# The vision-tower kernel: the row scatters wait for the values matmuls of their step

## The reference, cut to what matters

```python
h = einsum('bnd,ed->bne', patches, W) + b
a = layernorm(h)
q, k, v = split(a @ W_attn + b_attn)            # q and k get rotary factors
att = softmax(where(causal, q k^T * D**-0.5, -inf))
h = h + (att @ v) @ W_proj + b_proj
x = layernorm(h); t = rmsnorm(x) * norm_scale
top_vals, top_idx = top_k(t @ gate_w.T + gate_b, 4)
w = softmax(top_vals)
y_e = swiglu(t @ mlp1_w[e].T + mlp1_b[e]) @ mlp2_w[e].T + mlp2_b[e]
h = h + x + sum over the four experts e of w_e * y_e
```

## Time and profile before

| | |
|---|---|
| median of 3 runs | 541.59 us (537.69 to 542.88) |
| the profiled execution, its own time | 542.0 us |
| its span in the profile | 540.2 us |
| mean granted TensorE clock | 0.903 |
| busy: PE / DVE / ACT / POOL | 440.9 / 298.8 / 310.8 / 256.9 us |

### The profile page before, as it was taken

One profiled execution on the slowest core, in us unless ns is written; L12 is line 12 of the kernel. 1 busy time (PEld: TensorE's weight loads), 2 busy tenths in 40 slices (PEclk: granted clock), 3 DMA queues, 4 the chain that ended last, 5 costly groups with the idle time before them and its releaser, 6 DMA issues.

```text
span 540.2 us, 14340 instructions
## 1 busy us (share of the span) xinstructions
PE 440.9 (82%) x3865; PEld 390.1 (72%) x3866; DVE 298.8 (55%) x964; ACT 310.8 (58%) x832; POOL 256.9 (48%) x303
## 2 busy tenths in 40 slices
PE   2888977878787767119999999999999999999910
PEld 2676756556665545108999999999999999999910
DVE  0467968878778665403555555555555555555510
ACT  1247656666556642016777777777777777777600
POOL 1114576667677556700346444444444444444332
PEclk9789999999997755558999999999999999999965
DMA  8965454565541111333234444444344444432211
GB/s 222 257 158 166 138 152 147 172 172 153 153 134 51 41 41 56 128 114 101 52 55 78 61 63 61 63 61 61 53 69 61 61 61 62 63 40 30 24 22 22
DMA packets 41914, 49.72 MB, mean 92 GB/s; under 512 B 6387, under 2 KB 33251, under 8 KB 41860
## 3 DMA queue, kind: packets, MB, share of 16 engines
q1 hardware_dynamic: 26452, 33.48, 23.1%
q0 software_dynamic: 14544, 14.94, 17.9%
q10 hardware_dynamic: 864, 0.65, 0.4%
HBM read 30.82 MB, written 18.23 MB: 91 GB/s over the span
## 4 chain that ended last, share of the span: by engine, by line
PE 57%; issue 9%; DVE 9%; ACT 6%; another core or an unknown queue 5%; DMA 4%; SPq 4%; POOL 4%; POOLq 1%; DVEq 0%; ACTq 0%
PE bank L594 21%; PE bank L616 14%; PE bank L602 11%; PE bank L574 3%; PE bank L422 2%; ACT k_spread L657 2%; ACT p_spread L639 2%; POOL routed_rows L1140 2%; DMA out_rows<-x_sb 1%; SPq L322 1%; DMA x_sb<-patches 1%; SPq L321 1%; DVE t_row L902 1%; POOL rstd L1131 1%
## 5 line engine op out<-in xcount | busy, mean ns | idle before, releaser
L594 PE MATMUL bank<-rT,w_now 128*128 128x128 f32 x948 | 124.0, 281 | 0.3 <-ACT rT L639 0.3
L594 PEld LDWEIGHTS bank<-rT,w_now 128*128 128x128 f32 x948 | 115.1, 193 | 5.2 <-ACT rT L639 0.5
L730 ACT ACTIVATE k_spread<-bank,w_now 128x128 f32<-128x128 f32 x237 | 69.9, 372 | 58.1 <-PE bank L602 58.1
L1077 DVE TENSOR_TENSOR v_sb<-bank,w_now 128x384 f32<-128x384 f32 x79 | 44.1, 558 | 101.4 <-PE bank L602 80.4
L639 ACT ACTIVATE w_now<-w_sb 128x1158 f32 x79 | 92.5, 1171 | 13.4 <-issue 7.9
L616 PE MATMUL bank<-w_sb,p_spread 128*128 x474 | 83.9, 327 | 0.1
L1196 POOL DMA_INDIRECT out_rows<-x_sb,wtok_sb x25 | 40.1, 1605 | 79.9 <-issue 33.0
L616 PEld LDWEIGHTS bank<-w_sb,p_spread 128*128 128x128 f32 x474 | 76.1, 190 | 0.5 <-issue 0.4
L1140 POOL DMA_INDIRECT routed_rows<-packet,row_i x64 | 63.5, 992 | 24.2 <-issue 22.5
L602 PE MATMUL bank<-rT,w_now 64*128 64x128 f32 x948 | 64.2, 282 | 0.0
L1090 DVE SCALAR_TENSOR_TENSOR p_spread<-k_spread,v_sb 128x384 f32<-128x384 f32 x79 | 44.2, 560 | 35.7 <-ACT k_spread L730 31.4
(11 more groups left out here) (174 smaller groups left out, 688.6 us busy)
## 6 DMA issues: line engine op xcount, KB each, us to landing
x_sb<-patches SPq DMA_DIRECT2D x16, 384.0 KB, 3.4
w_sb<-w SPq DMA_DIRECT2D x32, 192.0 KB
w_sb<-w SPq DMA_DIRECT2D x16, 288.0 KB
w_sb<-w SPq DMA_DIRECT2D x64, 48.0 KB
wtok_sb<-routed_rows SPq DMA_DIRECT2D x25, 106.0 KB, 2.0
out_rows<-h SPq DMA_DIRECT2D x16, 96.0 KB
wproj_sb<-routed_rows SPq DMA_DIRECT2D x10, 106.0 KB
x_sb<-routed_rows SPq DMA_DIRECT2D x10, 106.0 KB
```

The source lines that it names most:

```text
L594: last = mm(dst[:, c * P:(c + 1) * P], w[:, a:a + P], t[:, part, :], start=(start and c == 0), stop=(not start and c == ICH - 1))
L730: last = nc.scalar.activation(gate_act[b][:, a:a + P], ps_glu[b][:, a:a + P], ACT.Silu, bias=w1_now[b][:, GLU_B + c:GLU_B + c + 1], scale= ...
L1077: V.tensor_tensor(lin[b].rearrange("p (c t) -> p c t", c=ICH), ps_lin[b][:, 0:INNER].rearrange("p (c t) -> p c t", c=ICH), w1_now[b][:, LI ...
```

## The change

POOL's instructions stay the same and in the same order. In the steps in which stages 6, 3 and 2 all hold a tile (n = 6 to 17, 12 of the 16 tiles' scatters), POOL waits, ahead of the first of the four scatters, for `pv_done` of the tile at stage 3: the values matmuls that PE runs in the same step.

```diff
                 if tile(6) is not None and tile(2) is not None:
+                    if tile(3) is not None:
+                        pool.wait_ge(s["pv_done"], tile(3) + 1)
                     scatter(tile(6), (n - 6) % 2)
                 if tile(4) is not None:
                     inverse_root(tile(4), ssq[:], 1.0 / DIM, "ssq_ready", msq, "msq_ready", rms, "t_row_ready",
                                  "rms_ready")
                     residual(tile(4))
```

## The result

The changed kernel takes 565.22 us (median of 4 runs, 563.68 to 566.96) against 541.57 us for the kernel before in the same session: +23.7 us, ratio 1.045, 95% interval 1.0388 to 1.0512. Slower, as forecast, and by more than the 14 us of the forecast, inside its range of 546 to 567. The profiled execution's span is 565.3 us, 25.1 more than before. In the table of runs further down a median is of all runs, while a ratio leaves out the slow ones, over 1.5% above the fastest of the same kernel: two of four in split_scatters and in changed_again (whose profile is of a slow one), one of four in split_again.

The account below looks back on a forecast made before the run. The step time was taken as bound by a loop of POOL's scatters, rms, DVE's t_row, inverse roots and row_i. First scatter at 65.61, eleven 12.71 us periods, +1.2 clock, -1.5 at the end: +14.2, 556 us, range 546 to 567.

Parts of the forecast that it names:

- Scatters, rms, t_row, pT, p_spread, values, scatters: Loop through POOL, DVE and PE that the new wait closes: 12.71 us a period, against 11.55 before.
- 4.86 + 0.92 + 0.1: Terms on POOL and DVE: four scatters 4.86 us, scatter end to rms end 0.92, rms end to t_row 0.1.
- the 5.09 from `t_row` to values: Terms t_row start to pT end 2.52 us, to first p_spread copy 0.32, four copies 2.10, then 0.15 to values.
- 0.92 + 0.82 = 1.74: Terms from PE to POOL: values to their signal 0.92 us, signal to first scatter 0.82.
- the clock term: Last changed steps at the lower clock: values to yT 1.56 us instead of 0.92, 1.2 us for two steps.
- the clock falls early: Rival: PE idles more and gets 1.2 GHz sooner, up to 1.2 us a step, 567 us in all; chance 0.10.
- A clock of 0.50 long before 165 us: Sign that the prediction is wrong: PE's clock at 0.50 well ahead of 165 us, from where it averaged 0.67.
- The loop's own bounds: Period of the token steps that the wait governs: 12.0 to 13.3 us, with 12.7 taken; chance 0.75.
- The lateness: Claim that scatters make PE's values signal late: 2.8 to 5.1 us to yT beside them, 0.92 without scatters.
- the 4.6 us of `p_pair`'s waits: POOL's p_pair waits 4.6 us in five steps for DVE's rinv_own; the change was to remove this.
- The shift of 1.7 us in step n = 6: First changed step: first scatter moves from 63.89 to 65.61 us, after values and their signal.
- The last step's gain of 1.5 us: Behind the last changed step, p_pair no longer waits 1.41 us for rinv_own; about 1.5 us given back.

Follow-up runs that it names:

- split_scatters: Kernel before, no wait, with two of the four scatters ahead of msq, rms and residual and two behind them in steps 6 to 17: 534.93 us, ratio 0.9852.
- changed_again: The changed kernel run once more, unaltered, for a second profile: 557.49 us, ratio 1.0522 to the kernel before.
- split_again: Repeat, on another chip, of the kernel before with two scatters ahead of rms and two behind residual, no wait: 534.33 us, ratio 0.9879.
- filled_pe: Changed kernel plus 8 extra unused PE matmuls ahead of the t_row transposes in steps 6 to 17: 554.57 us, ratio 1.0205 to the kernel before.
- scores_wait: Changed kernel with its wait on the earlier scores_done of stage 2 in place of pv_done: 546.12 us, ratio 1.0055 to the kernel before.
- split_filled: Kernel before with two scatters ahead of rms, two behind residual, no wait, plus 4 extra PE matmuls ahead of t_row's transposes: 520.82 us, ratio 0.9935.
- before_filled: Kernel before, no wait, with 8 extra PE matmuls ahead of the t_row transposes in steps 6 to 17: 552.15 us, ratio 1.0188.

## Why the prediction was right, and what it mis-sized

- **The direction and the loop: right.** "Scatters, rms, t_row, pT, p_spread, values, scatters", summed to 12.71 us. Shown: 12.4 us where the clock stays up (filled_pe), 12.8 in the changed kernel's faster steps. The terms 4.86 + 0.92 + 0.1 measure 5.81, the 5.09 from `t_row` to values 4.89, and 0.92 + 0.82 = 1.74 measures 1.71. Each was within 0.2 us.
- **What failed is the size of the clock term.** I gave 1.2 us for two steps at the end in the forecast itself, and 0.10 to the rival "the clock falls early", with up to 1.2 us a step. The clock fell in about every second step from n = 7 on, at 1.6 us a step where whole, 10.2 us in all by the comparison with filled_pe. A clock of 0.50 long before 165 us was one of the signs of being wrong, and it came. That rival's price (567) was nearer than the forecast (556). I had taken PE's mean busy share (0.83 to 0.73) and not where its idle time would stand: in one piece of 2.6 us ahead of the `t_row` transposes.
- **How much of the hit is luck.** The loop's own bounds, 12.0 to 13.3 us a period, end at about 563 us; the measured mean is 13.36 and the time 565.2. It lies in the range only because the upper end took in part of the clock rival. Term by term, the forecast's 14.2 us become the profile's 25.1 by 3.8 for the late start, 0.2 in step n = 6, -3.1 for the loop (12.4 for 12.7, eleven times), 9.0 for the clock (10.2 for 1.2) and 1.0 behind the last changed step: the loop's error hid part of the clock's.
- **The lateness: shown only in part.** With the scatters behind the values, `yT` comes 0.92 us after them (up to 1.57 where the clock is lower) in all 12 steps. In scores_wait the signal is 3.2 to 3.9 us behind the values in the 8 steps whose scatters start 0.3 to 0.5 us behind them, and 1.3 to 1.6 us in the 3 whose scatters start 1.0 us or more behind. So without scatters beside the values the signals are on time. But split_filled has the scatters beside the values and the signal on time, so the scatters alone do not make it late. What else it takes is open.
- **What the lateness costs the kernel before: misread.** The prediction says that the loop does not pass through the late signals in most steps, and prices them at the 4.6 us of `p_pair`'s waits. But DVE, which has `t_row`, works in order, and its base add waits for a late signal too. In the step after n = 7 of the kernel before:

```profile
80.00 0.57 POOL L1131 TENSOR_TENSOR rms<-msq,power 128x1 f32<-128x1 f32 x1
80.48 0.35 DVE L986 TENSOR_TENSOR h<-h,bank 128x192 f32<-128x192 f32 x1 [2.93 <-remote]
...
81.82 0.18 DVE L864 TENSOR_TENSOR rinv_own<-rinv,cst 128x24 f32<-128x24 f32 x1
...
82.06 0.75 DVE L902 SCALAR_TENSOR_TENSOR t_row<-x,rms,nscale_bc 128x192 f32<-128x192 f32 x1
```

  `t_row` starts 1.49 us behind the end of `rms`. It is 0.57 to 1.95 us late in 8 of the 12 steps and 0.1 or less in four (not three, as the prediction has it), 10.6 us in all; in the changed kernel it is 0.04 or less in every step. The periods of the kernel before are 10.8 to 11.2 us where `t_row` is on time, and 11.2 to 12.7 where it is not. An estimate: 127.0 us less eleven periods of 10.8 is 8 us that signals on time would be worth to this loop, and the wait costs more than that. The sum did not suffer, since it was built with every signal on time.
- **The shift of 1.7 us in step n = 6** measures 1.9. The four scatters take 4.98 us on average instead of 4.91, not the 0.2 to 0.7 us more that the prediction thought possible, and the expert phase is 1 us longer.
- **The last step's gain of 1.5 us**: from the last changed step's scatter to the end 0.5 us less was measured.
- **The rest of the difference**, 3.8 us ahead of the change's first effect, was no term of mine and is not explained.

## What to carry to other kernels

A wait put ahead of an instruction costs by the loop that it closes. Write down what is queued behind it on its engine and follow that until it comes back to what is awaited; every path counts, also the second longest (`p_pair` here). A late signal is worth neither the sum of the waits for it (here `yT` and the base add, 49 us) nor only the wait that the profile shows on the engine that sets the step (`p_pair`, 4.6 us): look also for work that merely stands behind a waiting instruction in its engine's order, here `t_row`, 10.6 us late in all. Where a change makes TensorE idle in one stretch each step, price the lower clock in the steps that follow; what helped here was not to wait but to cut the block of scatters in two (1.2 and 1.5% faster), so that what others wait for stands between the halves.

## What the runs showed of the hardware

- In most profiles TensorE's signals reach ACT and DVE late while POOL issues indirect DMAs: 2.8 to 5.1 us from values to `yT` in the first profile, 0.92 without scatters, and up to 5.4 with more matmuls in that time (before_filled). In split_filled they are on time, 0.92 us, with scatters in the same place; that run has four extra matmuls and was on another chip. Whether the matmuls or only their signals are late, no run here tells.
- An indirect DMA of 128 rows of 848 bytes holds POOL for 0.96 us, the first of four for 1.07, with 0.30 us to the next (at most 1.21 us in the first profile); the first of four starts 0.82 us after `row_i` ends.
- The clock fell to 1.2 GHz after TensorE had idled 2.6 us in the stretch from 126 to 130 us and came back some 13 us later; 8 useless matmuls a step, put into that gap, took about 10 us out of the periods.
- The same kernel took 525 us on one chip and 542 to 544 on others.
